# Matrix products without a reader in TensorE's waits, in a cross-attention, expert and product-key kernel

## What is computed

```python
x = x + _L0_xattn_ref(_layernorm(x), ctx_1024, ...)      # 16 heads, every 16th key row per head
x = x + _L0_ffn_ref(_layernorm(x), Wg, w1, w2)           # 16 experts, top 1, 256 places each
x = x + _L1_xattn_ref(_layernorm(x), ctx_1024, ctx_1024) # one head, causal mask, 77 keys
x = x + _L1_ffn_ref(_layernorm(x), ...)                  # dense SiLU part + 512 product-key experts
```

## Time and profile before

| | before |
|---|---|
| median of 3 runs | 506.21 us (505.69 to 508.18) |
| the profiled execution | 505.62 us, its span 503.9 us |
| mean granted TensorE clock over the span | 0.878 |
| busy, share of the span | TensorE 82%, VectorE 69%, ScalarE 62%, POOL 62% |
| HBM traffic | 54 GB/s over the span |

### The profile page before, as it was taken

One profiled execution on the slowest core, in us unless ns is written; L12 is line 12 of the kernel. 1 busy time (PEld: TensorE's weight loads), 2 busy tenths in 40 slices (PEclk: granted clock), 3 DMA queues, 4 the chain that ended last, 5 costly groups with the idle time before them and its releaser, 6 DMA issues.

```text
span 503.9 us, 8841 instructions
## 1 busy us (share of the span) xinstructions
PE 413.8 (82%) x2400; PEld 330.9 (66%) x2400; DVE 346.2 (69%) x1359; ACT 311.9 (62%) x792; POOL 310.3 (62%) x236
## 2 busy tenths in 40 slices
PE   4897888755999944969655899999998989989876
PEld 3786777624998943859422676777676766767666
DVE  3457777611232214798688999999999999899831
ACT  1443537241122212698743889899898998989845
POOL 5135867871000027573039789999989898998940
PEclk9577959776999995595777699999999999999999
DMA  6982000102576611120000000100001010100000
GB/s 197 354 222 79 33 21 22 43 31 62 153 222 198 179 42 53 35 86 27 1 10 1 21 23 32 33 31 21 10 31 31 31 31 31 31 31 21 12 12 21
DMA packets 42165, 31.84 MB, mean 63 GB/s; under 512 B 3899, under 2 KB 38299, under 8 KB 42139
## 3 DMA queue, kind: packets, MB, share of 16 engines
q1 hardware_dynamic: 38283, 24.95, 16.8%
q0 software_dynamic: 2624, 6.30, 3.7%
q10 hardware_dynamic: 1232, 0.31, 0.3%
HBM read 18.95 MB, written 8.39 MB: 54 GB/s over the span
## 4 chain that ended last, share of the span: by engine, by line
DVE 19%; ACT 14%; PE 11%; issue 7%; DVEq 1%; POOL 0%; ACTq 0%; POOLq 0%
ACT arena_sb L798 6%; DVE arena_sb L1623 6%; PE banks L1193 4%; DVE arena_sb L1601 3%; PE banks L1147 2%; PE banks L1202 2%; ACT L821 2%; DVE banks L1549 2%; DVE first_sb L1544 2%; DVE best_sb L1594 1%; PE banks L1178 1%; ACT banks L761 1%; ACT w_t_sb L559 1%; DVE first_sb L1564 1%; ACT summed_sb L812 1%
## 5 line engine op out<-in xcount | busy, mean ns | idle before, releaser
L523 POOL TENSOR_TENSOR arena_sb<-arena_sb 128x2144 f32<-128x2144 f32 x31 | 146.8, 4752 | 5.7 <-DVE arena_sb L1623 5.3
L1623 DVE SCALAR_TENSOR_TENSOR arena_sb<-arena_sb,best_sb,banks 128x536 f32<-128x536 f32 x124 | 87.4, 768 | 5.0 <-issue 2.5
L798 ACT ACTIVATE arena_sb<-arena_sb,bsum_sb 128x536 f32<-128x536 f32 x124 | 81.7, 733 | 0.2
L481 POOL DMA_INDIRECT arena_sb<-made,made_row_sb x32 | 30.9, 967 | 79.2 <-DMA made<-arena_sb 70.3
L513 POOL TENSOR_TENSOR arena_sb<-ex_sb,ey_sb 128x2048 f32<-128x2048 f32 x16 | 58.0, 3625 | 17.4 <-ACT banks L771 13.2
L1193 PEld LDWEIGHTS banks<-ident_sb,arena_sb 128*128 128x128 f32 x496 | 58.2, 153 | 13.0 <-ACT summed_sb L812 9.5
L1193 PE MATMUL banks<-ident_sb,arena_sb 128*128 128x128 f32 x496 | 61.5, 278 | 4.2 <-ACT summed_sb L812 4.2
L1147 PE MATMUL banks<-z_sb,xt_sb 128*128 128x512 f32 x64 | 37.0, 677 | 12.2 <-DVE arena_sb L1601 10.6
L1202 PE MATMUL banks<-up_e_sb,w_t_sb 128*128 128x128 f32 x256 | 35.4, 281 | 9.3 <-ACT w_t_sb L559 9.3
L1202 PEld LDWEIGHTS banks<-up_e_sb,w_t_sb 128*128 128x128 f32 x256 | 32.2, 191 | 13.2 <-ACT w_t_sb L559 12.4
L1433 DVE TENSOR_SCALAR arena_sb<-banks 128x512 f32<-128x512 f32 x16 | 11.1, 692 | 39.2 <-PE banks L1043 39.2
(11 more groups left out here) (189 smaller groups left out, 868.8 us busy)
## 6 DMA issues: line engine op xcount, KB each, us to landing
arena_sb<-w SPq DMA_DIRECT2D x32, 256.0 KB, 3.5
x_all_sb<-x SPq DMA_DIRECT2D x8, 256.0 KB, 3.3
slots<-arena_sb POOLq DMA_DIRECT2D x4, 512.0 KB, 8.5
arena_sb<-slots SPq DMA_DIRECT2D x16, 128.0 KB, 3.1
made<-arena_sb SPq DMA_DIRECT2D x16, 128.0 KB, 1.9
xt_sb<-x_t_sb SPq DMA_DIRECT2D x16, 128.0 KB, 2.0
xu_sb<-x_t_sb SPq DMA_DIRECT2D x16, 128.0 KB, 2.0
out<-x_all_sb SPq DMA_DIRECT2D x16, 128.0 KB, 1.8
```

The lines of the kernel that those rows point to most:

```text
L523: pool.tensor_tensor(prod[r][p], prod[r][p], table[r][p][:, :, 0:WIDE], ALU.mult).then_inc(weighed, 1)
L798: ins = act.activation(prod[r][p][:, h, :], prod[r][p][:, h, :], ACT.Silu, scale=bsum[r][:, n:n + 1])
L1623: ins = dve.scalar_tensor_tensor(out=prod[r][p][:, h, :], in0=table[r][p][:, h, 0:WIDE], scalar=best[r][:, n, TOP - 1:TOP], in1=scores_of( ...
```

## The change

A helper `warm(dst, n)` multiplies `ident` with the first n columns of `down_t` into a PSUM bank that is overwritten later without being read. It is called in TensorE's stream:

- before the loop over experts: once at once, twice after each second scatter of the last turn (four times two), once for each half of the last turn's `scattered` semaphores, and once more: 12 calls with 512 columns;
- before the middle stage: once after `y_ready`, once after each of the two `y_out`, twice after each second gather of group 0 (two times two), once with 256 columns after `gathered[0]`;
- in the first two groups: 256 columns after `tokens_t(0)`, 512 after `cmax_ready`, 512 after `gathered[1]`, 256 after `scores(1)`;
- once in every `last_tokens_t(g)`, between its two waits (eight times);
- once after `attention(7)` and once after `last_tokens_t(6)`.

POOL counts up a new semaphore `paced` after every second scatter of the last turn and after every second gather of group 0. Nothing is removed or moved.

```diff
@@ scatters
                     ).then_inc(scattered[i % 2][p], 16)
+                    if i == NI - 1 and t % 2:
+                        pool.sem_inc(paced, 1)
@@ gathers
                                             ).then_inc(gathered[g], 16)
+                    if g == 0 and n % 2:
+                        pool.sem_inc(paced, 1)
@@ TensorE
+            def warm(dst, n=512):
+
+                pe.matmul(dst[:, 0:n], ident[:, :], down_t[:, 0:n], start=True, stop=True)
@@ before the experts
             pe.wait_ge(loc_read, NI)
+            pe.wait_ge(wts_d, 64)
+            warm(bank[7])
+            for n in range(TT // 2):
+                pe.wait_ge(paced, n + 1)
+                warm(bank[7])
+                warm(bank[7])
+            for p in two:
+                pe.wait_ge(scattered[1][p], 16 * BT * (NI // 2))
+                warm(bank[7])
+            warm(bank[7])
@@ before the middle stage
             pe.wait_ge(ctx_in, 16)
+            warm(bank[7])
+            for p in two:
+                pe.wait_ge(y_out[p], 16 + 16 * (NE // 2))
+                warm(bank[7])
+            for n in range(BT // 2):
+                pe.wait_ge(paced, TT // 2 + n + 1)
+                warm(bank[7])
+                warm(bank[7])
+            pe.wait_ge(gathered[0], 16 * BT)
+            warm(bank[7], 256)
@@ last_tokens_t
                 pe.wait_ge(x3_ready, g + 1)
+                warm(bank[4 * p + 3])
                 pe.wait_ge(cxh_ready, g + 1)
@@ the groups
             tokens_t(0)
+            warm(bank[7], 256)
             scores(0)
+            pe.wait_ge(cmax_ready, 1)
+            warm(bank[7])
+            pe.wait_ge(gathered[1], 16 * BT)
+            warm(bank[7])
             tokens_t(1)
             probabilities_t(0)
             scores(1)
+            warm(bank[7], 256)
@@ the end of the groups
             attention(NB - 1)
+            warm(bank[0])
             last_tokens_t(NB - 2)
+            warm(bank[0])
```

More of the change, by code:

```diff
@@ L236, in program @@
         stored = sem("stored")
+        paced = sem("paced")
         late_picked, shared, last_own = sem("late_picked"), sem("shared"), sem("last_own")
```

## The result

The changed kernel takes 502.21 us (median of 6 runs, 501.12 to 504.89) against 505.84 us for the kernel before (median of 6, 504.69 to 508.18): a ratio of 0.9931, with a 95% interval of 0.9902 to 0.9959. Timed twice more, it came to 0.9955 [0.9926, 0.9984] and 0.9941 [0.9906, 0.9975]. Against the medians of the kernel before that were timed beside it, 505.48 and 505.46 us in the later two, it is faster by 3.6, 2.5 and 2.7 us. The forecast was 501.2 us, with a range of 498.6 to 504.2 us. A few executions run in a slower state, and the ratios leave them out; the only two among the edited kernels are one of `again2` and the profiled one of `fine`.

The account below looks back on a forecast made before the run. It took TensorE to bound the experts' stage and VectorE the groups. The terms 0.3 + 0.2 - 1.2 - 2.5 - 0.6 - 0.9 = -4.7 us on 505.6 us gave 500.9, set at 501.2 us, range 498.6 to 504.2 us.

Parts of the forecast that it names:

- POOL's counting: Increments between POOL's scatters and gathers cost 0.1 us each: +0.3 us ahead of the experts, +0.2 us for later gathers.
- Start of the experts: First transposes and hidden products run at the full clock, though five fillers delay them about 0.8 us: -1.2 us.
- First groups: Start of the middle stage: full-clock transposes and scores shorten VectorE's waits until gathers bound `combine(2)`: -2.5 us, the largest term.
- The other groups: From `combine(3)` to `combine(7)`, four periods go from 6.41 us to VectorE's own pace of 6.25 us: -0.6 us.
- the main number of the prediction: In the groups, 6.22 us per `combine` period at the half clock against 6.30 us at the full: VectorE bounds them.
- End of the middle stage: From `attention(7)` to `nears`, 6.9 us becomes 6.1 us at the full clock, fillers included: -0.9 us with rounding.
- The last stage: Nothing changes there but the phase of a clock that falls and rises until 287 us, +-1 us.
- sign of being right: From the experts to the middle stage's end, the granted clock is 1.00 from 106 us to about 257 us.
- lost between the stages: Rival: between the last expert's output and second gather only three fillers, clock falls, first group late; 503.2 us, chance 0.17.
- Cold groups: Rival: the clock falls in the groups despite fillers, each delaying six groups by 1.4 us; 510.6 us, chance 0.07.
- TensorE bounds the groups: Rival: the groups' period falls to VectorE's busy time of about 5.7 us; 498.5 us, chance 0.10.
- Nothing happens: Rival: the clock is not moved by the fillers' products anywhere; 506 us, chance 0.04.

Follow-up runs that it names:

- again2: The changed kernel run once more, unedited, for its time and a third profile: 502.77 us, 0.9941 of the kernel before.
- fine: Changed kernel with one filler per gather count of group 0, fewer ahead of `tokens_t(1)` and the experts, others moved or added: 500.08 us, 0.9884.
- only_counts: Changed kernel without any filler, keeping only POOL's increments of `paced`: 505.32 us, 0.9978 of the kernel before.
- best: `fine` with two more fillers behind the counts of the first gathers and a 256-column one in each group: 497.91 us, 0.9850 of the kernel before.
- again: The changed kernel run once more, unedited, for a second profile: 502.97 us, 0.9955 of the kernel before.
- loop3: Changed kernel with three fillers instead of one in `last_tokens_t`: 504.26 us, 0.9977 of the kernel before.
- no_loop: Changed kernel without the filler in `last_tokens_t`, all other fillers kept: 504.66 us, 0.9969 of the kernel before.
- only_loop: Changed kernel with only the filler in `last_tokens_t` kept, all other fillers dropped: 506.75 us, 1.0010 of the kernel before.

## Why the prediction came out as it did

The sign and the time were right. By its own steps:

- **POOL's counting, +0.5 us:** too dear. It is 0: the pauses around increments are 0.30 us, as everywhere, and `only_counts` shows nothing.
- **Start of the experts, -1.2 us:** the size was right, the way to it was not. The stage is 1.8 us shorter, and the row of fillers holds up its start by 0, 0.9 and 0.6 us in the three profiles of the changed kernel (forecast 0.8). But the prediction had "the last count" come with the end of the last scatter, and five fillers behind it. The last count came at 109.3 us, 5.5 us before that scatter's record began, and twelve fillers ran in one row from TensorE's own arrival on. That a row of 10.3 us from there ends about where five fillers behind the last scatter would have ended is luck. So is the hit on the first transposes, forecast near 119.4 us and come at 119.36: the stage before them was 0.7 us longer in this profile, and the hold-up of 0.8 us was missing.
- **First groups, -2.5 us:** this step failed in the profiles of the changed kernel, where it came out at +1.2, -1.8 and +1.2 us. The prediction took the clock there as full and wrote that the fillers "delay nothing on the path by more than their 0.43 us". That held the full fillers ahead of `tokens_t(1)` hidden at 0.9 us each; with the clock fallen they were 3.78 us and ended 2.3 us after the tokens they stood before were ready. The price of the term under its own condition was right: in the two executions of the same stream in which the clock held, `combine(0)` to `combine(2)` takes 10.24 and 10.23 us, 2.3 us less than before, and in `best` 10.00 us, 2.55 less. VectorE's longest wait for scores is 1.1 us in `best`, as forecast.
- **The other groups, -0.6 us:** right in kind, too small. It was -1.5, -0.8 and -1.5 us. The 6.30 us of the earlier trace rows, the main number of the prediction, is not VectorE's usual pace: with the clock full, four groups in five take 6.03 to 6.05 us. From `combine(4)` to `combine(5)` it takes 6.29 to 6.32 us in ten of the fourteen profiles, and that is the one pair with a full clock that the prediction read. Where VectorE goes from its first to its second batch of statistics it pauses there, in the kernel before as in the changed one, for what the profile puts down to nothing that was waited for:

```profile
220.74 0.87 DVE L1463 BATCH_NORM_STATS2 cbn_sb<-x_all_sb 128x6 f32<-128x128 f32 x4 [0.15 <-issue]
```

- **End of the middle stage, -0.9 us:** wrong in sign, +0.8 to +2.0 us. The clock was at half as the two fillers began (it fell at 245.9 and 244.3 us, in `again` at 241.5), and they cost up to double. With the full clock the sum was right: `loop3` gives 5.99 us without its two extra fillers, -0.9 us. The sentence that the third filler costs 0.9 us and that it would be -1.8 without it is borne out by `best`: 5.17 - 6.91 = -1.74 us.
- **The last stage:** unchanged, 250.3 to 250.5 us against 250.56 us.

The prediction's sign of being right, a clock of 1.00 from 106 to 257 us, did not come in any profile of the changed kernel. The rival "lost between the stages" (chance 0.17) names what its three profiles show, and at about the right place: few fillers between the last expert's output and the gathers, and a late first group. The reason it gave was short by one half. There are seven full fillers; the counts ran ahead of the gathers, and all were spent 2.3 us too early. Even then the fall is a matter of the execution, three in five. It gave 503.2 us; the medians are 502.2, 503.0 and 502.8 us. So the forecast's number came near partly by luck: the profiled executions gained 1.0 to 1.5 us behind the first stretch and not 4.7, and the median is near the forecast probably because other executions kept the clock. That is an inference from `no_loop` and `loop3`; no profile of the changed kernel shows such an execution.

"Cold groups" did not come: `only_loop` has its price of one cold filler, 0.75 us a group and not 1.4, but for one or two groups and not six. "TensorE bounds the groups" fell with `loop3`. "Nothing happens" fell with the clock, 0.878 to 0.941.

The rule of the Trainium skill that was weighed ("TensorE: Matmul & The Clock Gate", Part 4: PE-mode transpose), that the full clock does not engage for transposes, does not hold for these fp32 transposes: they kept a granted clock of 1.00 alone for 10.67 us. The measurement decides.

## What to carry to other kernels

A filler is free only while the clock it is meant to keep is still up: put it where the engine waits for something that comes later than twice the filler's length, never directly ahead of work that starts a stage. Look for the hole that is left behind the last filler: `best`, which all but closes it and takes fillers off the path, is another 4.9 us faster than the changed kernel timed beside it (497.91 against 502.77 us). A pace that a whole term rests on wants several periods, not one. And before a fall of the clock is called systematic, look at every profile that has the same stream up to that point, those of the other experiments too: three of one kernel agreed here, and two with the same instructions did not.

## What the runs showed of the hardware

- A semaphore count queued behind an indirect DMA on POOL came 0.97 us before that DMA's record began, while an earlier one was still under way. Behind eight scatters the last count came 5.5 us before the last record began (109.3 against 114.81 us). As a clock for another engine it runs ahead of the work. It cost POOL nothing.
- A rest of 2.34 to 2.40 us behind 6.67 us of products without a pause may or may not cost the clock: in three executions it fell, at 189.7 to 191.3 us, once during the rest and twice with TensorE already at work again, and in two it held for over 10 us more. In the two profiles of `best`, where the rest is 0.91 and 0.94 us, it held.
- Transposes held the clock for 10.7 us as products do.
- With the clock full, nothing late and at most one filler a group, a group takes 6.03 to 6.05 us, and the one from `combine(4)` to `combine(5)` 6.29 to 6.32 us, with a pause of VectorE ahead of its second batch of statistics. Why in this group alone stays open.
